# A decoder block in three interleaved stages: scores in one fp32 pass, key sums by a scan, other denominators, four strips, and a second copy of the context

## The reference

```python
x = x + attn(layernorm(x))               # 16 heads of 16, causal linear attention
x = x + xattn(layernorm(x), ctx, ctx)    # similarity of probabilities, softmax, MLP of 1024, layernorms
x = x + ffn(layernorm(x))                # top 128 tokens by router; causal softmax attention, gated MLP
# attn, per head, chunks of 128 tokens; phi = elu + 1
scores = where(mask, phi(q) @ phi(k).T, 0)
num = scores @ v + phi(q) @ S;   den = scores.sum(-1) + phi(q) @ z
S = S + phi(k).T @ v;            z = z + phi(k).sum(axis=tokens)
y = num / (den + 1e-6);          attn = concat(y) @ w_proj.T
# xattn: f = (v - softmax(-sid / 16) @ v) @ W_diff.T + b_diff + q, where v is the context
# ffn: att = softmax(causal(q @ k.T / 4)); o = att @ v
```

## Time and profile before

| what | value |
|---|---|
| time, median of 3 runs | 1065.25 us (1061.77 to 1066.12) |
| the profiled execution's own time | 1059.68 us |
| its span from the first to the last instruction | 1057.5 us |
| TensorE busy | 970.4 us, 92% |
| DVE, ACT, POOL busy | 685.9, 607.7, 283.7 us |
| mean granted clock of TensorE | 0.969 |

### The profile page before, as it was taken

How to read it: one execution, slowest core, us unless ns; L and a number is a source line. 1 busy time by engine, 2 the same in 40 slices (tenths; PEclk the granted TensorE clock), 3 DMA queues, 4 the chain that set the end, 5 groups by cost and what they waited for, 6 DMA issues and landing times.

```text
span 1057.5 us, 23674 instructions
## 1 busy us (share of the span) xinstructions
PE 970.4 (92%) x8576; PEld 852.5 (81%) x8576; DVE 685.9 (65%) x1637; ACT 607.7 (57%) x1357; POOL 283.7 (27%) x427
## 2 busy tenths in 40 slices
...
GB/s 257 77 8 20 2 21 1 31 2 10 20 10 20 10 20 0 30 0 16 14 10 20 10 20 0 30 0 30 0 10 20 10 20 11 10 3 11 1 10 11
DMA packets 15969, 21.22 MB, mean 20 GB/s; under 512 B 1216, under 2 KB 13504, under 8 KB 15936
## 3 DMA queue, kind: packets, MB, share of 16 engines
...
## 4 chain that ended last, share of the span: by engine, by line
PE 82%; ACT 6%; DVE 6%; issue 3%; DMA 2%; POOL 0%; SPq 0%; DVEq 0%; ACTq 0%; POOLq 0%
PE bank L1029 22%; PE bank L1257 8%; PE bank L1132 5%; PE bank L1152 5%; PE bank L1037 4%; PE bank L1327 3%; PE bank L1341 3%; PE bank L1302 3%; PE bank L1198 3%; PE bank L1352 3%; PE bank L1413 3%; PE bank L1224 3%; PE bank L1216 2%; ACT w_raw_or_stage_c L652 2%; PE bank L1290 2%
## 5 line engine op out<-in xcount | busy, mean ns | idle before, releaser
L617 ACT ACTIVATE prob<-bank,b_folded 128x256 f32<-128x256 f32 x128 | 53.4, 468 | 69.7 <-PE bank L1029 69.5
L652 ACT ACTIVATE w_raw_or_stage_c<-bank,c_nmax 128x128 f32<-128x128 f32 x256 | 71.3, 389 | 11.5 <-DVE c_nmax L955 11.5
L783 DVE TENSOR_TENSOR a_s<-bank,const 128x512 f32<-128x512 f32 x64 | 44.1, 688 | 43.1 <-PE bank L1132 23.5
L955 DVE TENSOR_REDUCE c_nmax<-bank 128x4 f32<-128x512 f32 x64 | 42.5, 686 | 38.6 <-PE bank L1327 38.6
L961 DVE RECIPROCAL c_rden_or_products<-bank 128x256 f32<-128x256 f32 x16 | 28.1, 1758 | 57.0 <-PE bank L1352 57.0
L490 ACT ACTIVATE b_s_hi<-prob 128x512 fp32r<-128x512 f32 x64 | 40.4, 632 | 37.7 <-PE bank L1257 37.1
L714 DVE TENSOR_TENSOR b_s_lo<-prob,b_s_hi 128x512 fp32r<-128x512 f32 x64 | 43.8, 685 | 20.2 <-ACT b_s_hi L490 20.2
L1029 PE MATMUL bank<-b_s_hi,w_mlp_hi 128*128 128x256 f32 x256 | 55.2, 297 | 0.8 <-DVE b_s_lo L714 0.6
L1152 PE MATMUL bank<-a_s,v_even 128*32 128x128 f32 x256 | 51.9, 285 | 4.1 <-DVE a_e L783 3.7
L1257 PE MATMUL bank<-w_mlp_hi,b_s_hi 128*128 128x256 f32 x256 | 52.2, 286 | 0.0
L1152 PE MATMUL bank<-a_e,v_even 128*32 128x128 f32 x256 | 51.8, 285 | 0.0
...
## 6 DMA issues: line engine op xcount, KB each, us to landing
...
```

Of the source, the lines that this page charges most:

```text
L617: act_in(prob[:, 2 * (j % 2) + n, :], b0[:, n * T:(n + 1) * T], ACT.Gelu, bias=b1p[:, f:f + 1]).then_inc(b_gelu.sem, 1)
L652: act_in(c_e[g % 2][:, j * R:(j + 1) * R], (c1, c2)[g % 2][:, j * R:(j + 1) * R], ACT.Exp, bias=c_nmax[:, n:n + 1]).then_inc(c_exp.sem, 1)
L783: tt(heads((a_s1, a_e0)[g % 2][:, :]), heads((a1, a2)[g % 2][:, :]), tri.unsqueeze(1).broadcast_to([P, 4, P]), ALU.mult).then_inc(a_scput. ...
L955: nc.vector.tensor_reduce(c_nmax[:, 4 * g:4 * g + 4], heads((c1, c2)[g % 2][:, :]), axis=AX.X, op=ALU.max, negate=True).then_inc(c_max.sem, 1)
```

## The change

It edits all three stages and the order.

1. Scores of stage a: one fp32 pass of `kT` against `qM`. The split of q and k and two of the four masked copies go.
2. Key sums by a running sum over tokens on DVE (`a_csum_`, two scans of 128x256). `a_ksum_` goes, and `a_ktp_`, `a_kput_` handle the first chunk alone, for `a_state_`. `a_den_` multiplies by a block of ones, so that the sum of a head stands on all its features. ACT adds the epsilon (`a_dput_`), DVE inverts 128x512 (`a_dinv_`). `a_rden_` and `a_rtp_` go.
3. Four buffers for masked scores; `a_att_t` runs twice a row over four strips.
4. The context is also passed turned, as `ctx_t`, and loaded into `b_f1` by one more DMA a row. `b_ctp_`, `b_ctput_` go.
5. Sums of stage c from the accumulator of the exps; `c_dinv_` (DVE, 128x16), `c_dbc_` (ACT spreads), `c_dtp_` (PE turns), `c_dput_` (ACT). Half of `c_att_` and the reciprocal of 128x256 go.
6. `ORDER` is another list, and `WEIGHTS_AT` has three splits before the first row, one later in iteration 0 and nine in iteration 1.

```diff
-WEIGHTS_AT = {(0, FIRST): 3} | {(0, f"a_scput_{g}"): 1 for g in range(1, 8)} | {(1, FIRST): 1, (1, "b_pnorm"): 1,
-              (1, "b_sid"): 1}
+WEIGHTS_AT = {(0, "c_etp_0"): 3, (0, "c_selu"): 1, (1, "c_score_1"): 1, (1, "c_max_3"): 1, (1, "c_etput_0"): 2, (1, "c_xo"): 1, (1, "c_mean"): 1, (1, "c_sbc"): 1, (1, "a_ktp"): 1, (1, "a_kq"): 1}
...
+            def next_ctx_t(b):
+                sp.wait_ge(*b_fd(b))
+                sp.sem_inc(passed.sem, 1)
+                sp.dma_start(b_f1[:, :, :], ctx_t_rows[b + 1]).then_inc(ctx_t_in.sem, 16)
...
             def a_dput_(b):
-                act_e.wait_ge(*a_rtp(b))
-                copy(a_e1[:, :], a0[:, :], a_dput)
+                act_e.wait_ge(*a_den(b))
+                act_in(a_e1[:, :], a0[:, :], ACT.Identity, bias=C["den_eps"]).then_inc(a_dput.sem, 1)
...
+                    if g == 0 and not first(b):
+                        act_e.wait_ge(*c_dinv(b - 1))
...
                         act_in(c_e[g % 2][:, j * R:(j + 1) * R], (c1, c2)[g % 2][:, j * R:(j + 1) * R], ACT.Exp,
-                               bias=c_nmax[:, n:n + 1]).then_inc(c_exp.sem, 1)
+                               bias=c_nmax[:, n:n + 1], accum_out=c_den[:, head:head + 1]).then_inc(c_exp.sem, 1)
...
+            def a_csum_(b):
+                dve.wait_ge(*a_phi(b))
+                for c in range(DC):
+                    nc.vector.tensor_tensor_scan(a_e1[:, c * T:(c + 1) * T], kT[:, c, :], kT[:, c, :], 0.0, ALU.add,
+                                                 ALU.max).then_inc(a_csum.sem, 1)
...
             def a_dinv_(b):
-                dve.wait_ge(*a_den(b))
-                ts(a_r[:, :], a0[:, 0:TT * NH], DEN_EPS, None, ALU.add).then_inc(a_dinv.sem, 1)
-                dve.wait_ge(*a_dinv(b, 1))
-                nc.vector.reciprocal(a_r[:, :], a_r[:, :]).then_inc(a_dinv.sem, 1)
+                dve.wait_ge(*a_dput(b))
+                nc.vector.reciprocal(a_e1[:, :], a_e1[:, :]).then_inc(a_dinv.sem, 1)
...
+            def c_dinv_(b):
+                dve.wait_ge(*c_exp(b))
+                nc.vector.reciprocal(c_rd[:, :], c_den[:, :]).then_inc(c_dinv.sem, 1)
...
             def a_den_(b):
                 pe.wait_ge(*a_kq(b))
-                for t in range(TT):
-                    for c in range(DC):
-                        last = mm(a0[:, t * NH + c * NH // DC:t * NH + (c + 1) * NH // DC],
-                                  a_e0[:, c * T + t * P:c * T + (t + 1) * P], C["chunk_heads"], start=True, stop=True)
+                pe.wait_ge(*a_vput(b))
+                for c in range(DC):
+                    last = mm(a0[:, c * T:(c + 1) * T], C["head_block"], a_e0[:, c * T:(c + 1) * T], start=True, stop=True)
...
                     for c in range(DC):
-                        for a, (p, q) in enumerate(PASSES):
-                            for n in groups:
-                                r = 32 * (n % 4)
-                                last = mm((a1, a2)[n % 2][:, 2 * c * P:2 * (c + 1) * P],
-                                          a_tr[p][r:r + 32, c, t * P:(t + 1) * P],
-                                          qM[q][r:r + 32, c, t, :, :].rearrange("p m q -> p (m q)"), start=a == 0,
-                                          stop=a == 2)
+                        for n in groups:
+                            r = 32 * (n % 4)
+                            last = mm((a1, a2)[n % 2][:, 2 * c * P:2 * (c + 1) * P], kT[r:r + 32, c, t * P:(t + 1) * P],
+                                      qM[r:r + 32, c, t, :, :].rearrange("p m q -> p (m q)"), start=True, stop=True)
...
                     for j, (c, m) in enumerate(GROUP):
-                        for n in groups:
-                            r = 32 * (n % 4)
+                        for n in range(4):
+                            r = 32 * n
                             last = mm(a0[r:r + 32, c * T + t * P:c * T + (t + 1) * P],
                                       vM[m][:, t, c * P + r:c * P + r + 32],
-                                      (a_s1, a_e0)[n % 2][:, j * P:(j + 1) * P], start=t == 0 and m == 0,
+                                      A_MASKED[n][:, j * P:(j + 1) * P], start=t == 0 and m == 0,
                                       stop=m == 1, skip_group_check=True)
...
             def b_v_(b):
-                pe.wait_ge(*b_ctput(b))
+                pe.wait_ge(*ctx_t_in(b))
```

More of the change, by code:

```diff
@@ L56 @@
+a_score_1 c_qkput c_max_1 b_orstd+
 """.split()
@@ L660, in c_etput_, with c_dbc_, c_dput_ @@
                 return step
+            def c_dbc_(b):
+                act_e.wait_ge(*c_dinv(b))
+                copy(c_rden[:, :].rearrange("p (h e) -> p h e", e=HD), c_rd[:, :].unsqueeze(2).broadcast_to([P, NH, HD]),
+                     c_dbc)
+            def c_dput_(b):
+                act_e.wait_ge(*c_dtp(b))
+                copy(c_rden[:, :], c2[:, 0:D], c_dput)
             def c_h2put_(b):
@@ L1081, in a_ktp_ @@
                 pe.wait_ge(*a_qout(b))
-                transposes(a1, kT, TT, DC).then_inc(a_ktp.sem, 1)
-            def a_ksum_(b):
-                pe.wait_ge(*a_kput(b))
-                pe.wait_ge(*a_vput(b))
-                for c in range(DC):
-                    cs = slice(c * P, (c + 1) * P)
-                    mm(a0[:, c * T:(c + 1) * T], k_tok[:, 0, cs], C["tri_ones"], start=True, stop=False)
-                    last = mm(a0[:, c * T + P:(c + 1) * T], k_tok[:, 1, cs], tri, start=False, stop=True)
-                last.then_inc(a_ksum.sem, 1)
+                transposes(a1, kT, 1, DC).then_inc(a_ktp.sem, 1)
             def a_state_(b):
@@ L1098, in a_state_ @@
                     cs = slice(c * P, (c + 1) * P)
-                    last = mm(a2[:, cs], k_tok[:, 0, cs], v0[:, cs], start=True, stop=True)
+                    last = mm(a2[:, cs], k_tok[:, cs], v0[:, cs], start=True, stop=True)
                 last.then_inc(a_state.sem, 1)
@@ L1203, in b_dtp_ @@
                 pe.wait_ge(*b_diff(b))
-                pe.wait_ge(*b_ctput(b))
+                if first(b):
+                    pe.wait_ge(b1_ready.sem, 1)
+                else:
+                    pe.wait_ge(*b_gelu(b - 1))
                 transposes(b0, b_f0, DC, TT).then_inc(b_pairtp.sem, 1)
@@ L1347, in c_att_, with c_dtp_ @@
                 for j, (c, m) in enumerate(GROUP):
-                    for den in range(2):
-                        for n in range(4):
-                            r = 32 * n
-                            lhs = den_ones[:, m, :] if den else cv[m][:, c * P + r:c * P + r + 32]
-                            last = mm(c1[r:r + 32, den * D + c * R:den * D + (c + 1) * R], lhs,
-                                      c_et[n][:, j * R:(j + 1) * R], start=j == 0 and den == 0, stop=m == 1,
-                                      skip_group_check=True)
-                last.then_inc(c_att.sem, 1)
+                    for n in range(4):
+                        r = 32 * n
+                        last = mm(c1[r:r + 32, c * R:(c + 1) * R], cv[m][:, c * P + r:c * P + r + 32],
+                                  c_et[n][:, j * R:(j + 1) * R], start=j == 0, stop=m == 1, skip_group_check=True)
+                last.then_inc(c_att.sem, 1)
+            def c_dtp_(b):
+                pe.wait_ge(*c_dbc(b))
+                for c in range(DC):
+                    last = nc.tensor.transpose(c2[:, c * R:(c + 1) * R], c_rden[:, c * P:(c + 1) * P], ident)
+                last.then_inc(c_dtp.sem, 1)
             def c_xo_(b):
                 pe.wait_ge(*c_selu(b))
-                pe.wait_ge(*c_exp(b))
+                pe.wait_ge(*c_dput(b))
                 for t in range(TT):
```

164 lines of the change are left out of this document (65 added, 99 removed).

## The result

The changed kernel takes 1023.17 us (median of 4 runs, 1022.43 to 1024.80), the kernel before 1063.51 in the same session. The ratio is 0.9627, with a 95% interval from 0.9588 to 0.9667. I forecast 980, in a range from 957 to 1012: the sign was right, the size was half of what I said. The profiled execution took 1024.80 us, with a span of 1022.9.

What follows compares the result with a forecast made beforehand. TensorE's own work was taken to bound the middle. Saving 5.06 us a row less 0.66 of new waits, 70 us over 16 rows, and 13 at the start gave 974 us of span, 980 as median, range 957 to 1012.

Steps and rivals of the forecast that it cites:

- TensorE's own work bounds the middle: From 240 to 840 us TensorE, busy for 592.3 of 600 us, sets the period of 58.98 us.
- rival 3: The four strips of `a_att` overlap worse than those of `c_att_`, 0.72 us more a row: 992 us, chance 0.05.
- 5.06: Us a row saved on TensorE: 4.70 of work and 0.36 of wait ahead of `b_v_`.
- New waits 0.66 us a period, between 0 and 3: All new waits together, at tight places such as the reciprocal, second `c_gtp` and `b_rtp_`; period then 54.6 us.
- the 56.5 that I had named as the sign of being wrong: A period above 56.5 us in the middle, where 54.6 was forecast, would show the forecast wrong.
- rival 1: More waits, as DVE's chains have less slack: 2.5 us a period instead of 0.66, time 1010 us, chance 0.22.
- the reciprocal's place: On DVE between the last masked scores and `c_o_`: 5.2 us of DVE work just covered by 5.6 on TensorE.
- Times 16 rows: The 4.4 us saved a period counts for 15 periods and one row beyond them: 70 us.
- The start: -13: Three weight splits instead of ten before the first row: 16.5 us earlier, 3 given back, net between -6 and -16.
- Rival 2: No waits, and the fp32 scores overlap into their neighbours: 5.06 + 0.68 us saved, time 956 us, chance 0.08.
- Rival 4: Slower: new DVE and ACT work, 6.4 to 9.1 us a row, stands in TensorE's way: 1073 us or more, chance 0.03.
- Rival 5: `b_v_` waits each row for the turned context's DMA on the one queue; folded into the case of more waits.

Runs made afterwards that it cites:

- ksum_short: The kernel before with `a_ksum_` cut from four matmuls to two of 32 columns: 1069.86 us, ratio 1.0068 to the kernel before.
- short_inverse: The changed kernel with the reciprocal of `a_dinv_` on 32 of its 512 columns: 1019.22 us, ratio 0.9585 to the kernel before.

## Why the prediction was wrong

- **"TensorE's own work bounds the middle": half true.** The chain of the earlier trace rows runs on TensorE, but there it had just enough work to cover DVE's run: at 14.02 and 13.58 us in 14.53 both engines were nearly full. I read the 0.76 us of idle time as slack for the whole period and never asked which other engine was full in a stretch. The Trainium skill (Perfetto Trace Analysis, Identifying the Most-Contended Engine) says to find the bottleneck by occupancy. By the occupancy of the whole span that is TensorE, at 92%, with DVE at 65%, and in the kernel before TensorE is ahead even inside that stretch. Still 1.0 us of its work was worth nothing there (ksum_short). The highest share alone didn't tell; how close the second one came did.
- **The terms: nearly right in size, but not in what they are worth.** `a_att` (1.9 us), the calls of the scores (1.07), `a_den_`, `c_dtp_` and the transposes that went measured as worked out; four strips cost what `c_att_` showed, so rival 3 is out. The sum came to 4.6 and not 5.06: `a_att_` without the state took 3.72 us before and not 3.96, since I had taken one call of 0.99 for all four, and `a_ktp_` with half the work takes 0.68, since the group behind it waits for DVE. Of the term `a_ksum_`, -1.61, ksum_short took off 1.0 us and got nothing, and the other 0.6 stands ahead of the same wait. That is shown in the old order; in the new one it is argued from DVE's run, which kept its length. Of the 5.06 us of my sum, 2.63 lies in DVE's run (`a_ksum_` 1.61, the context's transposes 0.44, half of `a_ktp_` 0.22, the wait ahead of `b_v_` 0.36), and that run went from 14.26 to 14.31. What the new order moved across its ends makes this sum a rough one.
- **The step that failed: "New waits 0.66 us a period, between 0 and 3".** On the groups that nobody touched it was 2.4, of which 1.44 stands at `c_gtp_` alone. The period was 2.2 us longer than forecast, 56.82 for 54.6, and past the 56.5 that I had named as the sign of being wrong: 1.8 of it is this term, the rest the terms above. I took the wait to be a small leftover behind the reciprocal. In these runs work cut from an engine that ran level with another turned into waits for the other, and that had to be the first case, not rival 1 with 0.22. Rival 1 has nearly the right figure (2.5), by luck and for the wrong reason: it named the reciprocal's place, which short_inverse cleared.
- **"Times 16 rows": wrong.** The saving shows in 13 periods, 28.3 us. Filling and draining the pipeline gave 6.3 us in place of my 13 for the start and 13 for three more rows.
- **The start: -13 was right for the spreading alone** (13.7 by medians), and the first transposes came at 15.79 as worked out. What I left out is that the new order needs 6.4 us more for row 0 with the same splits. With the periods this makes the 40 us.
- **The other rivals.** Rival 2 is out, since waits came. Rival 4 did not come: the reciprocal, its largest part, is covered. ksum_short was slower, but by the clock and not by exposed DVE work. Rival 5 did not come: nothing waits ahead of `b_v_`.
- **What stays open:** the 1.0 us a row on unchanged groups of the table is spread in pieces of 0.1 to 0.3. Some are waits too short to be printed, some may be what a product pays behind a group of another form; no run separates them.
